# One kernel, one change: the convolution's elementwise work divided anew between VectorE and GpSimd, and four half sums given to TensorE

## The chip, the cores and the metric

One core of a Trainium2 chip runs the whole program in one launch. The metric is the device time of one execution in microseconds; the profiled execution is one more of the same kind. Engine names as in the profile: PE is TensorE (PEld its weight loads), DVE VectorE, ACT ScalarE, POOL GpSimd, SP SyncE, which here only issues DMAs. Each engine works through its own list of instructions in order; semaphores order them across engines.

## What is computed

```
_layernorm(x): (x - mean) / sqrt(var + 1e-5)                    x: [8, 256, 512] fp32
v, x1, x2 = _layernorm(x), ctx, ctx      viewed as [8, 32 heads, 8, 512]
kv[i, j] = v[i] * x2[j]                  for each head: 8 x 8 products of rows
y  = causal convolution of kv with k[head] (512 taps)  +  kv * skip[head, i]
out[j] = sum_i y[i, j] * x1[i]
x = x + tanh(g_xattn) * out
x = x + tanh(g_ffn) * MoE(_layernorm(x))    8 experts, the best one per token, 512 -> 1024 -> 512
```

The second part (routing, sorting rows by expert, the experts' matmuls) is not touched by the change. The first, here called the convolution phase, is.

## The kernel before

The convolution phase works on G = 16 groups of 128 rows (8 batches x 16 rows, that is two heads hh = 0, 1 with J = 8 rows each, L = 512 long). After a transpose time lies on the partitions in LB = 4 blocks of 128. For each group g:

- ln1 (DVE, with a square root and the scaling on ACT), then v_in: PE transposes xn into v_bank (PSUM), and ACT's v_out copies it to vT.
- outer (L325, GpSimd): kv = all 8 x 8 products of a head, 128 x 2048. kv_high (L519, ACT) rounds it to kv_hi, kv_low (L621, DVE) makes kv_lo = kv - kv_hi.
- conv (L742, PE): for each head and output block lb, 3 (lb + 1) matmuls of 128 x 512 with the head's Toeplitz strips: 30 a head, 60 a group. kv_lo of a head has to be there before its first.
- product (L634, DVE): each finished block times cT into prod, eight slices i. Eight products a group.
- The sum over i: add_pairs (L462, GpSimd, once per head) halves eight slices to four, add_fours (L664, DVE) four to two, and sum_heads (L764, PE) adds the two and the skip term by accumulating transposes into att_bank: 3 x 4.
- The skip term: skip_first (GpSimd, two operations: v times skip L440, times cK L445) gives vc, skip_sum (L670, DVE) reduces it to skip_w, skip_last (L452, GpSimd) multiplies by cT into slice J of prod. vc and skip_w exist once, not per group parity.
- residual (L642), ln2, x2_in (PE transposes), logits_of, xn2_out: the second norm and the router's logits; xn_all keeps the normed rows for the experts.

Stage g of every engine's list is written by hand in stage(g, u, n), u = g mod 2: convolution and products of g stand beside the preparation of g + 1 (outer, kv_high, kv_low, skip_first) and the end of g - 1 (sum_heads, residual, ln2). ln1 runs two groups ahead. Stages 0, 1, 14 and 15 are unrolled, 2 to 13 are a loop.

SP's list: load_x(g + 2), load_cK(g + 1), load_cT(g), load_t(g + 1) (the 1 MB of strips of a group), the store of x2, x_res. A wait in one holds all that follow.

The strips are made on the chip: k is split in k_hi (ACT) and k_lo (k_low, DVE, L614), both go to DRAM as kparts, and make_strips (L299) expands them with overlapping reads, in three parts: group 0 (4 strips, issued by SP), groups 1 to 3 (12 strips) and groups 4 to 15 (48 strips, both issued by ACT). All three wait for the kparts writes (s_kout at 48). load_t takes part 0 for group 0, part 1 for groups 1 and 2, and inside the loop the last part, so from group 3 on.

## Time and profile before

| | us |
|---|---|
| median of 3 runs | 799.68 (796.83 to 801.11) |
| profiled execution | 799.75, span 797.5 |
| PE busy | 670.8 (84% of the span) |
| POOL busy | 617.8 (77%) |
| DVE busy | 527.9 (66%) |
| ACT busy | 241.9 (30%) |

Busy tenths in 40 slices of 20 us, and the share of the 16 DMA engines:

```profile
PE   1387779888888989986781989999999999999974
DVE  4259768777777777775742999559897983650400
ACT  4123313333333333322321222333233233223320
POOL 3399979999999999991273669779888886875862
DMA  4999375555554544410496676446666664541110
```

A digit is the busy share of its slice in tenths, 9 for 90% or more. The convolution phase is slices 1 to 19, the routing follows to about 430 us, the experts run to the end.

### The profile page before, as it was taken

The page shows a single profiled execution, that of the slowest core. Times are in us where ns is not written, and L with a number is a line of the kernel's source. Part 1 is how long each engine was busy: PE and PEld are TensorE (multiplying, and loading weights), DVE is VectorE, ACT ScalarE, POOL GpSimd, SP SyncE. Part 2 cuts the span into 40 slices and gives each one's busy share as a digit, 9 for nine tenths or more (in the row PEclk, how much of TensorE's full clock was granted, in tenths as well). Part 3 has the DMA queues.
Part 4 walks back from the last instruction along what each step waited for, and adds up shares of the span by engine and source line. Part 5 has one row for each costly group of instructions (what it writes and reads, how often), then busy time and mean ns, then how long its engine had stood idle before and what let it go on. Part 6 is the DMA issues. An engine that isn't in the chain of part 4 may idle for free.

```text
span 797.5 us, 11004 instructions
## 1 busy us (share of the span) xinstructions
PE 670.8 (84%) x3136; PEld 540.1 (68%) x3137; DVE 527.9 (66%) x661; ACT 241.9 (30%) x348; POOL 617.8 (77%) x373
## 2 busy tenths in 40 slices
PE   1387779888888989986781989999999999999974
PEld 0366668666666767765671767888788888888863
DVE  4259768777777777775742999559897983650400
ACT  4123313333333333322321222333233233223320
POOL 3399979999999999991273669779888886875862
PEclk9998889999999999998696899999999999999996
DMA  4999375555554544410496676446666664541110
GB/s 136 353 347 312 133 213 145 145 145 145 145 145 145 145 145 132 118 55 26 157 223 171 231 246 222 172 143 201 208 231 201 198 223 128 188 132 41 50 51 6
DMA packets 58462, 130.63 MB, mean 164 GB/s; under 512 B 5932, under 2 KB 6124, under 8 KB 58448
## 3 DMA queue, kind: packets, MB, share of 16 engines
q1 hardware_dynamic: 43108, 96.87, 38.8%
q10 hardware_dynamic: 11020, 20.99, 8.1%
q0 software_dynamic: 4320, 12.60, 6.0%
q8 instruction: 7, 0.11, 0.1%
q14 instruction: 7, 0.06, 0.0%
HBM read 111.11 MB, written 37.67 MB: 187 GB/s over the span
## 4 chain that ended last, share of the span: by engine, by line
PE 36%; DVE 7%; POOL 3%; issue 3%; DMA 2%; ACT 0%; DVEq 0%; POOLq 0%; ACTq 0%
PE pair L1197 21%; PE bank L1210 12%; POOL sorted_x L937 2%; PE bank L1230 2%; DMA sorted_x<-xn_all,pos 1%; DVE up L1023 1%; DVE down_hi L1023 1%; DVE down_lo L1026 1%; DVE gate L1023 1%; DVE up L1026 1%; PE bank L1186 1%; DVE gate L1026 1%; DMA raw<-down_w 1%; DVE select L876 0%; POOL ys L1131 0%
## 5 line engine op out<-in xcount | busy, mean ns | idle before, releaser
L742 PE MATMUL bank<-kv_hi,strip 128*128 128x512 f32 x640 | 222.4, 415 | 24.2 <-DMA strip<-strips 22.3
L742 PEld LDWEIGHTS bank<-kv_hi,strip 128*128 128x128 f32 x640 | 125.4, 196 | 55.1 <-issue 26.2
L325 POOL TENSOR_TENSOR kv<-vT,cK 128x2048 f32<-128x2048 f32 x31 | 156.1, 5036 | 0.0
L742 PE MATMUL bank<-kv_lo,strip 128*128 128x512 f32 x320 | 131.0, 409 | 0.0
L621 DVE TENSOR_TENSOR kv_lo<-kv,kv_hi 128x2048 fp32r<-128x2048 f32 x32 | 81.5, 2548 | 51.6 <-ACT kv_hi L519 51.5
L462 POOL TENSOR_TENSOR prod<-prod 128x1024 f32<-128x1024 f32 x31 | 107.5, 3487 | 4.7 <-DVE prod L634 4.7
L1197 PE MATMUL pair<-gate,xT_hi 128*128 x304 | 98.9, 407 | 5.0 <-DVE xT_lo L1032 2.8
L1197 PE MATMUL pair<-up,xT_hi 128*128 x304 | 96.7, 399 | 2.8 <-DVE up L1026 2.8
L634 DVE TENSOR_TENSOR prod<-bank,cT 128x512 f32<-128x512 f32 x128 | 82.1, 681 | 25.4 <-DMA cT<-ctx_cols 20.7
L1023 DVE CAST down_hi<-raw 128x1024 fp32r<-128x1024 f32 x32 | 34.2, 1068 | 73.7 <-PE bank L1210 50.5
L519 ACT ACTIVATE kv_hi<-kv 128x2048 fp32r<-128x2048 f32 x32 | 61.3, 1916 | 65.8 <-POOL kv L325 54.8
L1148 POOL TENSOR_TENSOR hid<-hid,mid 128x1024 f32<-128x1024 f32 x19 | 50.1, 2638 | 31.5 <-ACT mid L1077 31.4
L742 PEld LDWEIGHTS bank<-kv_lo,strip 128*128 128x128 f32 x320 | 62.8, 196 | 11.8
L1197 PEld LDWEIGHTS pair<-up,xT_hi 128*128 128x128 f32 x304 | 57.8, 191 | 17.1 <-issue 3.2
L1197 PEld LDWEIGHTS pair<-gate,xT_hi 128*128 128x128 f32 x304 | 56.9, 192 | 18.4 <-issue 5.8
L1210 PE MATMUL bank<-down_hi,hT_hi 128*128 128x512 f32 x152 | 62.9, 414 | 6.4 <-POOL hT_lo L1158 5.7
L1210 PE MATMUL bank<-down_hi,hT_lo 128*128 128x512 f32 x152 | 61.1, 402 | 0.0
L1210 PE MATMUL bank<-down_lo,hT_hi 128*128 128x512 f32 x152 | 61.0, 401 | 0.0
L1197 PE MATMUL pair<-gate,xT_lo 128*128 x152 | 60.9, 401 | 0.0
L1197 PE MATMUL pair<-up,xT_lo 128*128 x152 | 60.6, 399 | 0.0
L1026 DVE TENSOR_TENSOR down_lo<-raw,down_hi 128x1024 fp32r<-128x1024 f32 x32 | 56.3, 1758 | 1.1
L1131 POOL TENSOR_TENSOR ys<-ys,x2s 128x512 f32<-128x512 f32 x19 | 33.5, 1761 | 25.8 <-ACT ys L1070 25.8
(149 smaller groups left out, 1131.1 us busy)
## 6 DMA issues: line engine op xcount, KB each, us to landing
strip<-strips SPq DMA_DIRECT2D x16, 1024.0 KB, 5.7
raw<-gate_w SPq DMA_DIRECT2D x32, 512.0 KB, 4.1
raw<-up_w SPq DMA_DIRECT2D x32, 512.0 KB, 4.4
raw<-down_w SPq DMA_DIRECT2D x32, 512.0 KB, 4.3
strips<-kparts ACTq DMA_DIRECT2D x1, 12288.0 KB, 74.7
sorted_x<-fill SPq DMA_DIRECT2D x14, 513.0 KB, 6.0
xs<-sorted_x ACTq DMA_DIRECT2D x20, 256.5 KB
x_in<-x_rows SPq DMA_DIRECT2D x16, 256.0 KB, 5.5
```

The lines of the kernel that those rows point to most:

```text
L325: engine.tensor_tensor(kv[:, hh, :].rearrange("p (a i j) -> p a i j", i=J, j=J), v.unsqueeze(3).broadcast_to([P, LB * NB, J, J]), c.unsque ...
L462: nc.gpsimd.tensor_tensor(terms[:, 0:J // 2], terms[:, 0:J // 2], terms[:, J // 2:J], ALU.add)\
L519: nc.scalar.activation(kv_hi[:, u, hh, :], kv[:, hh, :], ACT.Copy).then_inc(s_khi, 1)
L621: nc.vector.tensor_tensor(kv_lo[:, u, hh, :], kv[:, hh, :], kv_hi[:, u, hh, :].bitcast(f32), ALU.subtract).then_inc(s_klo, 1)
L634: nc.vector.tensor_tensor(dst[:, :, :, hh * J:(hh + 1) * J], y_bank[lb][:, :].rearrange("p (b i j) -> p b i j", i=J, j=J), c, ALU.mult).th ...
L742: last = nc.tensor.matmul(y_bank[lb][:, :], strip[:, u, 2 * hh + t, d * P:(d + 1) * P], v[:, u, hh, mb * COL:(mb + 1) * COL], start=(mb == ...
L1023: nc.vector.tensor_copy(hi, raw[:, c, :]).then_inc(s_whi, 1)
L1026: nc.vector.tensor_tensor(lo, raw[:, c, :], hi.bitcast(f32), ALU.subtract)\
L1131: nc.gpsimd.tensor_tensor(ys[:, :], ys[:, :], x2s[:, :], ALU.add).then_inc(s_add, 1)
L1148: nc.gpsimd.tensor_tensor(hid[:, :], hid[:, :], mid[:, :], ALU.mult).then_inc(s_hid, 1)
L1197: last = nc.tensor.matmul(bank[:, half * 512:(half + 1) * 512], a[:, b, :], weights[:, bass.ds(o, 512)], start=(b == 0 and n == 0), stop=( ...
L1210: last = nc.tensor.matmul(out_bank[:, :], a[:, b, :], w[:, b * 512:(b + 1) * 512], start=(b == 0 and n == 0), stop=(b == IB - 1 and n == 2))
```

## The change

kv_low goes from DVE to GpSimd; outer goes from GpSimd to DVE and reads v_bank in PSUM, so vT and v_out are gone. skip_first becomes one operation per head that reads the diagonal of kv. add_pairs is one operation for both heads, add_fours is gone, and sum_heads takes slices 0 to 3 and J: 5 x 4 transposes. skip_last(g - 1) and add_pairs(g - 1) both stand at the head of GpSimd's stage g; skip_sum(g) stands in DVE's stage g ahead of the outers of g + 1. k_low comes after both first norms. xn2 is kept twice and xn2T_out, xn2_out, ln1, v_in and x2_in change places.

```diff
-    xn2 = put("xn2", [P, L], f32, att)
+    xn2 = put("xn2", [P, 2, L], f32, att)
     xn2T = put("xn2T", [P, LB, P], f32, att)
-    vT = put("vT", [P, 2, LB * P], f32, att)
...
-        def outer_product(engine, u, hh):
...
                 def load_cK(g, u):
                     wait(eng, s_kv, 2 * (g - 1))
-                    wait(eng, s_skip, g - 1)
...
-                def outer(g, u, n, hh):
+                def skip_first(g, u, hh):
                     h = 2 * g + hh
-                    if hh == 0:
-                        eng.wait_ge(s_vT, g + 1)
-                        eng.wait_ge(s_cK[u], 16 * (n + 1))
-                    wait(eng, s_khi, h - 1)
-                    wait(eng, s_klo, h - 1)
-                    outer_product(nc.gpsimd, u, hh)
-                def skip_first(g, u):
-                    a = LB * NB
+                    eng.wait_ge(s_kv, h + 1)
                     wait(eng, s_skw, g)
-                    wait(eng, s_skip, g)
-                    s_g = skip_b[:, blk(g, 2 * J)]
-                    nc.gpsimd.tensor_tensor(
-                        vc[:, :].rearrange("p (a r) -> p a r", r=2 * J),
-                        vT[:, u, :].rearrange("p (a r) -> p a r", r=2 * J),
-                        s_g.unsqueeze(1).broadcast_to([P, a, 2 * J]), ALU.mult).then_inc(s_skv, 1)
-                    eng.wait_ge(s_skv, g + 1)
-                    nc.gpsimd.tensor_tensor(vc[:, :], vc[:, :], cK[:, u, :], ALU.mult).then_inc(s_skip, 1)
+                    v = vc[:, :].rearrange("p (a r) -> p a r", r=2 * J)[:, :, hh * J:(hh + 1) * J]
+                    same = kv[:, hh, :].rearrange("p (a d) -> p a d", d=J * J)[:, :, ::J + 1]
+                    s_g = skip_b[:, blk(g, 2 * J)][:, hh * J:(hh + 1) * J]
+                    nc.gpsimd.tensor_tensor(v, same, s_g.unsqueeze(1).broadcast_to([P, LB * NB, J]), ALU.mult)\
+                        .then_inc(s_skip, 1)
+                def kv_low(g, u, hh):
+                    h = 2 * g + hh
+                    eng.wait_ge(s_khi, h + 1)
+                    wait(eng, s_y, (h - 3) * LB)
+                    nc.gpsimd.tensor_tensor(kv_lo[:, u, hh, :], kv[:, hh, :], kv_hi[:, u, hh, :].bitcast(f32),
+                                            ALU.subtract).then_inc(s_klo, 1)
                 def skip_last(g, u, n):
...
                         skip_w[:, :, :].unsqueeze(3).broadcast_to([P, LB * NB, 2, J]), ALU.mult)\
                         .then_inc(s_skp, 1)
-                def add_pairs(g, u, hh):
-                    eng.wait_ge(s_p, (2 * g + hh + 1) * LB)
-                    terms = prod[:, u, 0:J, :].rearrange("p i (a r) -> p i a r", r=2 * J)[:, :, :, hh * J:(hh + 1) * J]
+                def add_pairs(g, u):
+                    eng.wait_ge(s_p, (g + 1) * 2 * LB)
+                    nc.gpsimd.tensor_tensor(prod[:, u, 0:J // 2, :], prod[:, u, 0:J // 2, :],
+                                            prod[:, u, J // 2:J, :], ALU.add).then_inc(s_add, 1)
+                def add_first_pairs(g, u):
+                    eng.wait_ge(s_p, g * 2 * LB + LB)
+                    terms = prod[:, u, 0:J, :].rearrange("p i (a r) -> p i a r", r=2 * J)[:, :, :, 0:J]
                     nc.gpsimd.tensor_tensor(terms[:, 0:J // 2], terms[:, 0:J // 2], terms[:, J // 2:J], ALU.add)\
                         .then_inc(s_add, 1)
-                def before_conv(g, u, n):
-                    if isinstance(g, int) and g == 0:
-                        eng.wait_ge(s_small, 32)
-                        eng.wait_ge(s_kv, 1)
-                    else:
-                        outer(g, u, n, 0)
-                    skip_first(g, u)
-                    outer(g, u, n, 1)
+                def before_conv(g, u):
+                    for hh in range(2):
+                        if isinstance(g, int) and g == 0 and hh == 0:
+                            eng.wait_ge(s_small, 32)
+                        skip_first(g, u, hh)
+                        kv_low(g, u, hh)
                 def stage(g, u, n):
                     if known(g, lambda g: g >= 1):
-                        add_pairs(g - 1, 1 - u, 1)
-                    skip_last(g, u, n)
+                        add_pairs(g - 1, 1 - u)
+                        skip_last(g - 1, 1 - u, n - 1 + u)
                     if known(g, lambda g: g < G - 1):
-                        before_conv(g + 1, 1 - u, n + u)
-                    add_pairs(g, u, 0)
-                before_conv(0, 0, 0)
+                        before_conv(g + 1, 1 - u)
+                before_conv(0, 0)
                 stages(eng, stage)
+                skip_last(G - 1, 1, G // 2 - 1)
+                add_first_pairs(G - 1, 1)
...
                 def norm2(g, u):
                     act.wait_ge(s_nb2, g + 1)
-                    wait(act, s_x2tr, g)
-                    wait(act, s_xnc, g)
-                    norm(xn2[:, :], x_res[:, u, :], rs2, nb2, s_xn2)
+                    wait(act, s_x2tr, g - 1)
+                    wait(act, s_xnc, g - 1)
+                    norm(xn2[:, u, :], x_res[:, u, :], rs2, nb2, s_xn2)
+                def xn2_out(g, u):
+                    act.wait_ge(s_xn2, g + 1)
+                    nc.scalar.activation(xn_all[:, blk(g), 0:L].rearrange("p o n -> p (o n)"), xn2[:, u, :],
+                                         ACT.Copy).then_inc(s_xnc, 1)
                 def k_high():
                     act.wait_ge(s_kin, 16)
                     nc.scalar.activation(k_hi[:, :], k_raw[:, :], ACT.Copy).then_inc(s_khalf, 1)
-                def v_out(g, u):
-                    act.wait_ge(s_vtr, g + 1)
-                    wait(act, s_kv, 2 * (g - 1))
-                    wait(act, s_skip, g - 1)
-                    nc.scalar.activation(vT[:, u, :], v_bank, ACT.Copy).then_inc(s_vT, 1)
...
                 def stage(g, u, n):
                     more = known(g, lambda g: g < G - 1)
                     before = known(g, lambda g: g >= 1)
-                    if known(g, lambda g: g < G - 2):
-                        root1(g + 2)
-                        norm1(g + 2, u)
+                    if known(g, lambda g: g >= 2):
+                        xn2T_out(g - 2)
                     if more:
                         kv_high(g + 1, 1 - u, 0)
                     if known(g, lambda g: g >= 2):
                         logits_out(g - 2)
+                    if more:
+                        kv_high(g + 1, 1 - u, 1)
                     if before:
                         root2(g - 1)
                         norm2(g - 1, 1 - u)
-                    if more:
-                        kv_high(g + 1, 1 - u, 1)
                     if known(g, lambda g: g < G - 2):
-                        v_out(g + 2, u)
+                        root1(g + 2)
+                        norm1(g + 2, u)
                     if before:
-                        xn2_out(g - 1)
-                        xn2T_out(g - 1)
...
+                def outer(g, u, n, hh):
                     h = 2 * g + hh
-                    dve.wait_ge(s_khi, h + 1)
-                    wait(dve, s_y, (h - 3) * LB)
-                    nc.vector.tensor_tensor(kv_lo[:, u, hh, :], kv[:, hh, :], kv_hi[:, u, hh, :].bitcast(f32),
-                                            ALU.subtract).then_inc(s_klo, 1)
+                    if hh == 0:
+                        dve.wait_ge(s_vtr, g + 1)
+                        dve.wait_ge(s_cK[u], 16 * (n + 1))
+                    wait(dve, s_khi, h - 1)
+                    wait(dve, s_klo, h - 1)
+                    wait(dve, s_skip, h - 1)
+                    v = v_bank.rearrange("p (a r) -> p a r", r=2 * J)[:, :, hh * J:(hh + 1) * J]
+                    c = cK[:, u, :].rearrange("p (a r) -> p a r", r=2 * J)[:, :, hh * J:(hh + 1) * J]
+                    nc.vector.tensor_tensor(
+                        kv[:, hh, :].rearrange("p (a i j) -> p a i j", i=J, j=J),
+                        v.unsqueeze(3).broadcast_to([P, LB * NB, J, J]),
+                        c.unsqueeze(2).broadcast_to([P, LB * NB, J, J]), ALU.mult).then_inc(s_kv, 1)
...
-                def add_fours(g, u):
-                    dve.wait_ge(s_add, 2 * (g + 1))
-                    nc.vector.tensor_tensor(prod[:, u, 0:2, :], prod[:, u, 0:2, :], prod[:, u, 2:4, :], ALU.add)\
-                        .then_inc(s_add2, 1)
                 def skip_sum(g):
-                    dve.wait_ge(s_skip, g + 1)
+                    dve.wait_ge(s_skip, 2 * (g + 1))
                     wait(dve, s_skp, g)
                     nc.vector.tensor_reduce(skip_w[:, :, :],
                                             vc[:, :].rearrange("p (a h i) -> p a h i", h=2, i=J), AX, ALU.add)\
...
                     before = known(g, lambda g: g >= 1)
                     product(g, u, n, 0, 0)
                     product(g, u, n, 0, 1)
-                    if before:
-                        add_fours(g - 1, 1 - u)
-                    if known(g, lambda g: g < G - 2):
-                        ln1(g + 2, u, n + 1)
+                    skip_sum(g)
+                    if more:
+                        outer(g + 1, 1 - u, n + u, 0)
                     product(g, u, n, 0, 2)
+                    if more:
+                        outer(g + 1, 1 - u, n + u, 1)
                     product(g, u, n, 0, 3)
                     if before:
                         residual(g - 1, 1 - u, n - 1 + u)
                         ln2_first(g - 1, 1 - u)
-                    if more:
-                        kv_low(g + 1, 1 - u, 0)
-                    if before:
                         ln2_last(g - 1)
                     product(g, u, n, 1, 0)
+                    if known(g, lambda g: g < G - 2):
+                        ln1(g + 2, u, n + 1)
                     product(g, u, n, 1, 1)
-                    if more:
-                        skip_sum(g + 1)
                     product(g, u, n, 1, 2)
                     product(g, u, n, 1, 3)
-                    if more:
-                        kv_low(g + 1, 1 - u, 1)
-                k_low()
                 ln1(0, 0, 0)
                 ln1(1, 1, 0)
-                dve.wait_ge(s_vT, 1)
-                dve.wait_ge(s_cK[0], 16)
-                outer_product(nc.vector, 0, 0)
-                kv_low(0, 0, 0)
-                skip_sum(0)
-                kv_low(0, 0, 1)
+                k_low()
+                outer(0, 0, 0, 0)
+                outer(0, 0, 0, 1)
                 dve.wait_ge(s_tanh, 2)
                 stages(dve, stage)
                 add_last_pairs(G - 1, 1)
-                add_fours(G - 1, 1)
...
-                    wait(pe, s_vT, g)
-                    transposes(v_bank, xn, s_vtr)
+                    wait(pe, s_kv, 2 * g)
+                    transposes(v_bank, lambda cols: xn[:, cols], s_vtr)
...
-                    pe.wait_ge(s_add2, g + 1)
+                    pe.wait_ge(s_add, G + 1 if isinstance(g, int) and g == G - 1 else g + 1)
                     pe.wait_ge(s_skp, g + 1)
                     wait(pe, s_x2, g)
-                    terms = [0, 1, J]
+                    terms = [0, 1, 2, 3, J]
...
-                    conv(g, u, n, 1, (0, 1, 2))
+                    conv(g, u, n, 1, range(LB))
                     if known(g, lambda g: g < G - 2):
                         v_in(g + 2)
-                    conv(g, u, n, 1, (3,))
                     if before:
-                        x2_in(g - 1)
+                        x2_in(g - 1, 1 - u)
```

## Rows read from the trace of the kernel before

**Rows 1.** Timeline of GpSimd, one group: start us, us, engine line op, operands, count.

```profile
169.72 1.08 POOL L452 TENSOR_TENSOR prod<-cT,skip_w 128x512 f32<-128x512 f32 x1
...
175.44 1.30 POOL L440 TENSOR_TENSOR vc<-vT,skip_b 128x512 f32<-128x512 f32 x1
...
178.06 5.78 POOL L325 TENSOR_TENSOR kv<-vT,cK 128x2048 f32<-128x2048 f32 x1
183.80 6.75 POOL L462 TENSOR_TENSOR prod<-prod 128x1024 f32<-128x1024 f32 x2
190.51 1.08 POOL L452 TENSOR_TENSOR prod<-cT,skip_w 128x512 f32<-128x512 f32 x1
```

**Rows 2.** Timeline of SP's queue, the start of the convolution phase.

```profile
4.10 0.36 SPq L393 DMA_DIRECT2D kparts<-k_lo  x1
...
7.24 0.77 SPq L299 DMA_DIRECT2D strips<-kparts  x1
21.40 0.38 SPq L357 DMA_DIRECT2D strip<-strips  x1
...
37.37 0.38 SPq L357 DMA_DIRECT2D strip<-strips  x1
...
91.03 0.38 SPq L357 DMA_DIRECT2D strip<-strips  x1
```

**Rows 3.** Timeline of ACT, its issue of strips parts 1 and 2.

```profile
14.65 7.97 ACTq L299 DMA_DIRECT2D strips<-kparts  x2
```

**Rows 4.** Timeline of DVE, 0 to 115 us; in brackets the idle time before and its releaser.

```profile
12.20 0.21 DVE L604 TENSOR_SCALAR nb<-mv,rs 128x1 f32<-128x1 f32 x1
...
36.57 1.29 DVE L634 TENSOR_TENSOR prod<-bank,cT 128x512 f32<-128x512 f32 x2 [9.20 <-DMA cT<-ctx_cols]
...
58.12 1.29 DVE L634 TENSOR_TENSOR prod<-bank,cT 128x512 f32<-128x512 f32 x2 [3.89 <-DMA cT<-ctx_cols]
...
106.28 1.29 DVE L634 TENSOR_TENSOR prod<-bank,cT 128x512 f32<-128x512 f32 x2 [7.66 <-DMA cT<-ctx_cols]
```

**Rows 5.** Four lines, each by itself: count, duration in ns (min/median/max), first and last start.

```profile
L1158 POOL TENSOR_TENSOR hT_lo<-mid,hT_hi x19: 2346/2407/3295, 442.3 to 776.5; 128x1024 fp32r<-128x1024 f32 x19
...
L325 POOL TENSOR_TENSOR kv<-vT,cK x31: 3722/4719/5788, 17.3 to 344.3; 128x2048 f32<-128x2048 f32 x31
L325 DVE TENSOR_TENSOR kv<-vT,cK x1: 2284/2284/2284, 12.3 to 12.3; 128x2048 f32<-128x2048 f32 x1
...
L519 ACT ACTIVATE kv_hi<-kv x32: 1899/1918/1926, 14.6 to 350.1; 128x2048 fp32r<-128x2048 f32 x32
...
L670 DVE TENSOR_REDUCE skip_w<-vc x16: 670/676/679, 19.4 to 347.9; 128x64 f32<-128x512 f32 x16
```

**Rows 6.** Timeline of DVE beside rows 1.

```profile
177.65 2.60 DVE L621 TENSOR_TENSOR kv_lo<-kv,kv_hi 128x2048 fp32r<-128x2048 f32 x1 [0.96 <-ACT kv_hi L519]
```

**Rows 7.** Timeline of PE: transposes, 18 matmuls, transposes.

```profile
82.97 1.48 PE L764 MATMUL pair<-ident,prod 128*128 128x128 f32 x12
84.20 0.48 PE L742 MATMUL bank<-kv_hi,strip 128*128 128x512 f32 x1
...
88.49 0.60 PE L722 MATMUL pair<-ident,xn 128*128 128x128 f32 x4
```

**Rows 8.** Windows: length, busy us of five engines, then PE clock, DMA share, GB/s.

```profile
12.00:16.00 4.00, 1.11 (x4) 0.71 (x4) 2.58 (x3) 2.17 (x2) 1.23 (x1) 1.00 0.26 100
85.00:90.00 5.00, 5.00 (x25) 4.08 (x24) 3.95 (x7) 2.07 (x3) 4.92 (x4) 1.00 0.15 58
```

**Rows 9.** Timeline of DVE, the end of the convolution phase.

```profile
367.54 0.69 DVE L634 TENSOR_TENSOR prod<-bank,cT 128x512 f32<-128x512 f32 x1 [2.13 <-PE bank L742]
...
369.60 1.22 DVE L664 TENSOR_TENSOR prod<-prod 128x1024 f32<-128x1024 f32 x1
```

**Rows 10.** Timeline of PE, the same stretch.

```profile
370.88 2.26 PE L764 MATMUL pair<-ident,prod 128*128 128x128 f32 x12 [1.19 <-DVE prod L664]
```

**Rows 11.** Timeline of ACT, the same stretch.

```profile
380.49 0.62 ACT L538 ACTIVATE xn_all<-xn 128x512 f32<-128x512 f32 x1
```

More of the change, by code:

```diff
@@ L534, in xn2T_out @@
                         .then_inc(s_xn2T, 1)
-                def xn2_out(g):
-                    act.wait_ge(s_xn2, g + 1)
-                    nc.scalar.activation(xn_all[:, blk(g), 0:L].rearrange("p o n -> p (o n)"), xn2[:, :], ACT.Copy)\
-                        .then_inc(s_xnc, 1)
                 def stage(g, u, n):
@@ L569, in _ @@
                 norm1(0, 0)
-                v_out(0, 0)
                 root1(1)
@@ L573, in _ @@
                 kv_high(0, 0, 0)
-                v_out(1, 1)
                 make_strips(act, 1)
@@ L578, in _ @@
                 stages(act, stage)
+                xn2T_out(G - 2)
                 logits_out(G - 2)
@@ L582, in _ @@
                 xn2T_out(G - 1)
+                xn2_out(G - 1, 1)
                 logits_out(G - 1)
-                xn2_out(G - 1)
             @block.vector
```

22 lines of the change are left out of this document (7 added, 15 removed).

## The prediction

> **What bounds the kernel now.** I read the page's busy shares and slices first: PE is busiest, and the chain that ended last is PE almost throughout from 500 us on, but none of that is code that the change touches. The change lies in the convolution phase, up to 381 us, so I read the timeline of each engine there. GpSimd (POOL) never stops in the loop: an add_pairs for each head, skip_last, outer, two vc products, outer, and again, every 20.79 us (190.51 less 169.72) [rows 1]. So a group costs what GpSimd's queue costs.
>
> The loop doesn't run freely from the start. Before it stand DMAs: the expanded strips are written to DRAM in three parts, part 0 issued by SP at 7.24 and landed at 21.40, when SP goes on to load strip(0); parts 1 and 2 issued by ACT from 14.65; part 2 landed at 91.03, when SP goes on to strip(3) [rows 2, 3]. Behind strip(3) in SP's queue stands cT(3), and DVE starts group 3's products with it at 106.28 [rows 4]. From there GpSimd sets the time of 12 groups (3 to 15).
>
> **GpSimd's new queue.** It loses two outers and two vc products of 512, and gets two kv_low of 2048 and two skip_first of 256 elements a partition; its two add_pairs of 1024 become one of 2048. Durations: a 1024-element GpSimd subtraction takes 2.35 when nothing delays it, 512 take 1.30 [rows 1, 5], so 2.1 ns an element and 0.2 fixed: 4.52 for 2048, about 4.48 from start to next start; 256 elements 0.70. Bounds for 2048: 3.72 (the outer, with broadcast operands) and 5.79 (its longest) [rows 5]; the 1024 row is the very operation of kv_low, so I go by it. New queue: 3 x 4.48 + 1.08 + 2 x 0.70 = 15.9 us a group, 4.9 less than now.
>
> Is the undelayed duration the right one? The outer takes 3.72 or up to 5.79, and the long one at 178.06 runs into DVE's kv_lo (177.65 for 2.60, alone 2.28): 178.06 to 180.25 is overlap, and 3.6 is left [rows 1, 5, 6]. So one waits for the other. After the change DVE has no operation in the loop with two SBUF inputs left: outer and product each take one from PSUM. The Trainium skill (SBUF — State Buffer, "Who interferes with whom") says the same: a DVE instruction with two SBUF inputs and a GpSimd one that reads SBUF exclude each other, one with a single SBUF input excludes nobody. The trace agrees.
>
> **Why 15.9 isn't the period.** DVE's skip_sum(g) overwrites skip_w, so it waits for s_skp at g: skip_last(g-1). In the old code GpSimd does skip_last(g) at the start of stage g; now add_pairs(g-1) and skip_last(g-1) both stand in stage g, add_pairs first. And skip_sum(g) is now ahead of both outers of the next group in DVE's queue. That closes a ring over three engines. From the start of add_pairs(g-1), called A: add_pairs 4.48, skip_last 1.08; skip_sum 0.59 (0.68, less the overlap with what follows); outer for head 0 at 2.28 (the one that DVE does now; it reads SBUF, but a product from PSUM is no slower than its size: two of 512 in 1.29); kv_high 1.92; then kv_low 4.48, skip_first 0.70, kv_low 4.48, and the next add_pairs [rows 1, 4, 5]. Three hand-overs between engines are 0.21 in all, an estimate (one from DVE to PE is 0.06: add_fours ends at 370.82, PE starts at 370.88 [rows 9, 10]). Sum 20.22 us. GpSimd idles some 4.3 of it, waiting for kv_high of head 0. The new period is 20.22 against 20.79: 0.57 x 11 = 6.3 us, not the 54 that the queue alone would promise.
>
> Other engines in this ring: DVE after skip_sum has two outers, two products, residual, two norms and four products, some 13 us, so it ends near A + 19, inside the period. PE: 18 matmuls take 4.29, so 60 take 14.3; twelve transposes take 1.23, so twenty 2.05; with two sets of four transposes (0.6 at most each) and the logits about 18 us [rows 7]. The eight added transposes (0.8 us) vanish in PE's idle time. sum_heads comes about 6.2 after A and finds skip_last done at 5.6. Dropping add_fours frees DVE and takes away a wait of PE, but neither is in the ring: nothing gained there. ACT loses v_out and has room.
>
> Bounds of the period: skip_first reads the diagonal of kv with a step of 36 bytes, which no GpSimd row shows; nearest are 0.70 by size and 1.30 as for 512. The Trainium skill (GPSIMD Engine Reference, "Performance pitfalls for Q7 kernels") speaks against it: reads with a step over 8 bytes cost about one cycle an element more. By it 256 elements would add about 0.2 us (an estimate), 11 groups 2.3 us, and the sum below would be 801.3. No run here shows it. For the period I keep both ends: 17.9 (2048 elements at 3.72) and 21.0 (skip_first 1.3, outer 2.5); the long end of 5.79 is the exclusion, which is gone.
>
> **The start, where the change gives time back.** k_low is moved on DVE from the very front to behind ln1(0) and ln1(1). Those wait for ACT's first square root; the last of ln1(1) starts at 12.20 now, and without ACT's v_out ahead of the second square root at about 10.7, an estimate; its ends are 10 and 12.2. So k_low runs at 10.8, SP's kparts<-k_lo goes from 4.10 to 11.5, and make_strips(0), 3.14 behind it, from 7.24 to 14.66 [rows 2, 4]: 7.4 late. ACT's parts 1 and 2 wait for the same but left at 14.65 anyway [rows 3]: unmoved. Part 0 now competes from its first byte.
>
> What that is worth hangs on the DMA engines. While part 0 runs alone the share is 0.26 at 100 GB/s, four of 16 engines; at the end of part 2, 85 to 90 us, the share is 0.15: two or three engines work on while the others are done [rows 8]. If the last ones are part 0's four, the work they don't do before 14.66 comes at their end, and 91.03 becomes 98.4. The Trainium skill (DMA: Bandwidth & Descriptors, "Why a DMA increments its semaphore by 16 and not by 1") has the rule: a transfer whose slowest dimension is 4 or 12 long uses the lowest-numbered 4 or 12 engines. By it the last are part 0's; otherwise nothing shifts. The trace's 0.26 and its straggling end agree with the rule. I take the shift: cT(3) and the products of group 3 at 106.28 + 7.42 = 113.7, the next skip_sum could start at 114.9 (two products, 1.21).
>
> There is a second way to be late. Part 0 lands later: alone it took 14.2 us from issue, which would be 28.8; at half rate it is 37. I take 35.5. SP's strip(0), x_in, cK, cT follow: 15.2 us from SP's issue to the first product now (21.40 to 36.57), 20.7 when the engines are full (37.37 to 58.12, with one load more) [rows 2, 4]. I take 17.5: the first product at 53.0 instead of 36.6. From there the ring runs: 1.21, then skip_sum to second kv_low 14.63, two periods 40.4, add_pairs and skip_last 5.6: skip_last(2) ends 61.8 later, at 114.8. Both ways meet at 114.9. (Today there is slack here: DVE waits 7.66 us for cT(3) [rows 4].) Then add_pairs(3) starts at 114.9 + 14.63 = 129.5.
>
> **The sum.** Eleven periods: add_pairs(14) at 129.5 + 222.4 = 351.9; skip_last(14) ends at 357.5; sum_heads(14) 2.05 to 359.6; the last 30 matmuls 7.15; the last product starts at 366.9 instead of 367.54 [rows 9]. Tail: add_fours 1.2 less; eight more transposes at the pace of that place (twelve took 2.26) 1.5 more; ACT's xn2_out, 0.62, goes ahead of logits_out and leaves the end, 0.5 less [rows 9 to 11]: -0.2. Together -0.8. The rest of the program is unchanged. The profiled execution took 799.75 us around a span of 797.5, close to the median of 799.68, so the forecast is **799.0 us**: no change, the gain of the period (6.3, and about 2 from the first cycle) eaten by the start.
>
> **Rivals.**
> - Faster, the start is free: the straggling engines are others, and part 0 lands before 28. Then group 3 begins at 106.28 as now, which needs the first product by 45.6; add_pairs(3) at 122.1, and the time is 791.6. For it: the strip loads have slack of tens of us now. Against: share 0.26 and the thin end of the transfer. 0.17.
> - Faster, PE is the bound: skip_last isn't what skip_sum waits for in time. PE's 18.2 a group instead of 20.2 gives 799.0 - 11 x 2.0 = 777. The code's order speaks against it. 0.04; a ring that is shorter because GpSimd's 2048s take 4.1 would be 3 x 0.38 x 11 = 13 less, 786. 0.06.
> - Slower, the start: SP's first loads, in the full DMA. If part 0 lands at 38 and cT(0) 20.7 behind it, the first product is at 58.7, skip_last(2) ends at 120.5 and everything is 5.6 later: 804.6. It decides from a first product at about 57.2, when it passes 803. 0.17.
> - Slower, the ring: the strided skip_first at 1.3 and an outer from PSUM at 2.5 give 21.0, 11 x 0.8 = 9 more: 808. It decides from 20.6. 0.10.
>
> **How the numbers follow.** What can be told from no change here is 0.5%, 4 us. The forecast's case, 795.5 to 803 by itself, holds 0.46. Faster by over 0.5%: 0.27; within: 0.46; slower: 0.27. The range of 8 in 10 reaches to the first and third rival and half into the fourth: 791 to 807.
>
> **What would show it.** In the changed profile: DVE idle before skip_sum, ended by GpSimd's skip_last, some 4 us in each group; GpSimd idle 2.9 before the first skip_first, ended by DVE's outer, and 1.4 before the first kv_low, ended by ACT; periods of 20.2 between add_pairs; GpSimd's 2048s at 4.5 with little spread; SP's part 0 at 14.7, part 2 landed at 98; the first product near 53; the last near 367. I am wrong if add_pairs come every 18 us (the ring isn't closed), if group 3's products start at 106 (the start is free), or if kv_low stretches well over 4.6.

## The result, and the profile after

The changed kernel takes 806.65 us (median of 12 runs, 804.81 to 808.59) against 798.75 for the kernel before (12 runs, 796.80 to 804.24): ratio 1.0094, 95% interval 1.0075 to 1.0113. The forecast was 799.0, "no change". The time lies just inside the upper end of the range, 791 to 807, but the kernel became slower, by 0.9%, and that is clear of the measurement's uncertainty where the forecast had said no change.

The profiled execution of the changed kernel took 805.02 around a span of 802.9. Its busy times and the count of instructions (page, part 1; span in the first line):

```profile
span 802.9 us, 11207 instructions
...
PE 677.2 (84%) x3264; PEld 554.8 (69%) x3265; DVE 485.9 (61%) x644; ACT 238.2 (30%) x332; POOL 558.3 (70%) x359
```

PE's 3264 matmuls hold the 128 added transposes (16 groups of 8; with 12 a group there are 3136). No engine is full in the convolution phase. What fills a group is read from the timelines. GpSimd, one group (counterpart of [rows 1]; in brackets idle time before the operation and who ended it):

```profile
234.06 4.63 POOL L444 TENSOR_TENSOR prod<-prod 128x2048 f32<-128x2048 f32 x1
238.59 1.15 POOL L435 TENSOR_TENSOR prod<-cT,skip_w 128x512 f32<-128x512 f32 x1
242.91 0.91 POOL L420 TENSOR_TENSOR vc<-kv,skip_b 128x256 f32<-128x256 f32 x1 [3.17 <-DVE kv L608]
244.94 4.63 POOL L427 TENSOR_TENSOR kv_lo<-kv,kv_hi 128x2048 fp32r<-128x2048 f32 x1 [1.12 <-ACT kv_hi L506]
249.52 0.82 POOL L420 TENSOR_TENSOR vc<-kv,skip_b 128x256 f32<-128x256 f32 x1
250.30 4.56 POOL L427 TENSOR_TENSOR kv_lo<-kv,kv_hi 128x2048 fp32r<-128x2048 f32 x1
254.83 4.58 POOL L444 TENSOR_TENSOR prod<-prod 128x2048 f32<-128x2048 f32 x1
```

DVE beside it (counterpart of [rows 6]):

```profile
239.84 0.69 DVE L653 TENSOR_REDUCE skip_w<-vc 128x64 f32<-128x512 f32 x1 [4.61 <-POOL prod L435]
240.45 2.28 DVE L608 TENSOR_TENSOR kv<-pair,cK 128x2048 f32<-128x2048 f32 x1
...
250.92 1.88 DVE L623 TENSOR_TENSOR prod<-bank,cT 128x512 f32<-128x512 f32 x3
```

The last row holds the last three products of the group; they end at 252.80. ACT beside it:

```profile
242.85 1.93 ACT L506 ACTIVATE kv_hi<-kv 128x2048 fp32r<-128x2048 f32 x1 [9.81 <-DVE kv L608]
```

Follow the releasers: skip_sum (239.84) had to wait 4.61 us for skip_last; GpSimd's skip_first (242.91) for DVE's outer; kv_low (244.94) for ACT's kv_high. So the ring of the forecast is closed, with GpSimd idle for 4.29 us of it (3.17 + 1.12; forecast 4.3), and a group takes 254.83 - 234.06 = 20.77 us: as much as before (20.79). DVE's waits say how often (engine, line, waited for: us, times, longest):

```profile
DVE skip_w L653 <- POOL prod L435: 63.6, 15, 7.4
```

The start. SP's queue (counterpart of [rows 2]):

```profile
13.37 0.77 SPq L296 DMA_DIRECT2D strips<-kparts  x1
...
97.94 0.38 SPq L344 DMA_DIRECT2D strip<-strips  x1
```

DVE there (counterpart of [rows 4]):

```profile
11.05 0.67 DVE L594 TENSOR_TENSOR k_lo<-k_raw,k_hi 32x512 fp32r<-32x512 f32 x1
...
52.09 1.29 DVE L623 TENSOR_TENSOR prod<-bank,cT 128x512 f32<-128x512 f32 x2 [35.98 <-DMA cT<-ctx_cols]
...
112.42 1.29 DVE L623 TENSOR_TENSOR prod<-bank,cT 128x512 f32<-128x512 f32 x2 [5.04 <-DMA cT<-ctx_cols]
115.29 0.69 DVE L653 TENSOR_REDUCE skip_w<-vc 128x64 f32<-128x512 f32 x1 [1.57 <-POOL prod L435]
```

k_low runs at 11.05 and what stands behind it is late: strips part 0 by 6.1 us, strip(3) by 6.9, group 3's first product by 6.1 (106.28 before). But these products are not what holds group 3 up: skip_sum(3), at 115.29, has waited 1.57 us more for skip_last(2), the end of the second group's way round the ring. The end of the phase, DVE (counterpart of [rows 9]):

```profile
373.58 0.69 DVE L623 TENSOR_TENSOR prod<-bank,cT 128x512 f32<-128x512 f32 x1 [2.13 <-PE bank L716]
```

PE there (counterpart of [rows 10]):

```profile
375.66 2.40 PE L738 MATMUL pair<-ident,prod 128*128 128x128 f32 x20
```

The last product is 6.0 us later than the 367.54 of before, the routing behind it 4.4 (it starts at 385.83, against 381.43), and the span is 5.4 longer. The medians are 7.9 apart: the profiled execution of the changed kernel (805.02) is a quick one of its runs, that of before (799.75) is not. Windows around those transposes (length; busy us of PE, PEld, DVE, ACT, POOL; PE clock, DMA share, GB/s), in the changed kernel:

```profile
375.60:378.10 2.50, 2.46 (x22) 2.20 (x21) 0.00 (x2) 0.18 (x1) 0.00 (x0) 1.00 0.00 0
```

In the kernel before:

```profile
370.80:373.20 2.40, 2.26 (x12) 1.86 (x12) 0.04 (x2) 0.00 (x0) 0.00 (x0) 0.65 0.00 0
```

Twenty transposes at the full granted clock (2.4 GHz) take 2.40 us; twelve took 2.26 with the granted clock at 0.65 over the stretch, so between its two levels.

### The profile page after: what moved, and what is told of

Read it like the earlier page. It is cut to its first block, busy times and chain, and to the rows that moved or that the text cites. A ratio compares the mean times of both kernels' runs of the same rounds, so it can differ in the third digit from the quotient of the medians.

```text
span 802.9 us, 11207 instructions
## 1 busy us (share of the span) xinstructions
PE 677.2 (84%) x3264; PEld 554.8 (69%) x3265; DVE 485.9 (61%) x644; ACT 238.2 (30%) x332; POOL 558.3 (70%) x359
## 4 chain that ended last, share of the span: by engine, by line
PE 36%; DVE 7%; POOL 3%; issue 2%; DMA 2%; ACT 0%; POOLq 0%; DVEq 0%; ACTq 0%
PE pair L1170 22%; PE bank L1183 12%; POOL sorted_x L910 2%; PE bank L1203 2%; DMA sorted_x<-xn_all,pos 1%; DVE up L999 1%; DVE up L996 1%; DVE down_hi L996 1%; DVE down_lo L999 1%; PE bank L1159 1%; DVE gate L999 1%; DVE gate L996 1%; DMA raw<-down_w 1%; DVE select L849 0%; POOL ys L1104 0%
## 5 line engine op out<-in xcount | busy, mean ns | idle before, releaser
L716 PE MATMUL bank<-kv_hi,strip 128*128 128x512 f32 x640 | 216.7, 409 | 30.7 <-DMA strip<-strips 30.7
L427 POOL TENSOR_TENSOR kv_lo<-kv,kv_hi 128x2048 fp32r<-128x2048 f32 x32 | 147.3, 4602 | 23.1 <-ACT kv_hi L506 19.7
L623 DVE TENSOR_TENSOR prod<-bank,cT 128x512 f32<-128x512 f32 x128 | 84.6, 684 | 75.0 <-DMA cT<-ctx_cols 43.4
L1170 PE MATMUL pair<-gate,xT_hi 128*128 x304 | 101.1, 415 | 4.8 <-DVE xT_lo L1005 2.6
L420 POOL TENSOR_TENSOR vc<-kv,skip_b 128x256 f32<-128x256 f32 x32 | 28.3, 883 | 80.4 <-DVE kv L608 67.5
L608 DVE TENSOR_TENSOR kv<-pair,cK 128x2048 f32<-128x2048 f32 x32 | 72.9, 2281 | 0.0
L1170 PEld LDWEIGHTS pair<-gate,xT_hi 128*128 128x128 f32 x304 | 58.3, 197 | 18.6 <-issue 5.6
L1170 PEld LDWEIGHTS pair<-up,xT_hi 128*128 128x128 f32 x304 | 57.8, 191 | 17.2 <-issue 3.2
L444 POOL TENSOR_TENSOR prod<-prod 128x2048 f32<-128x2048 f32 x15 | 69.1, 4604 | 0.0
L696 PE MATMUL pair<-ident,xn 128*128 128x128 f32 x128 | 21.2, 313 | 46.1 <-ACT xn L480 41.3
```

The source lines that it names most:

```text
L420: nc.gpsimd.tensor_tensor(v, same, s_g.unsqueeze(1).broadcast_to([P, LB * NB, J]), ALU.mult)\
L427: nc.gpsimd.tensor_tensor(kv_lo[:, u, hh, :], kv[:, hh, :], kv_hi[:, u, hh, :].bitcast(f32), ALU.subtract).then_inc(s_klo, 1)
L444: nc.gpsimd.tensor_tensor(prod[:, u, 0:J // 2, :], prod[:, u, 0:J // 2, :], prod[:, u, J // 2:J, :], ALU.add).then_inc(s_add, 1)
L608: nc.vector.tensor_tensor(kv[:, hh, :].rearrange("p (a i j) -> p a i j", i=J, j=J), v.unsqueeze(3).broadcast_to([P, LB * NB, J, J]), c.uns ...
L623: nc.vector.tensor_tensor(dst[:, :, :, hh * J:(hh + 1) * J], y_bank[lb][:, :].rearrange("p (b i j) -> p b i j", i=J, j=J), c, ALU.mult).th ...
L716: last = nc.tensor.matmul(y_bank[lb][:, :], strip[:, u, 2 * hh + t, d * P:(d + 1) * P], v[:, u, hh, mb * COL:(mb + 1) * COL], start=(mb == ...
```

## The experiments

Theory: two separate things. **Ring**: skip_last behind add_pairs closes the ring, which costs what GpSimd's shorter queue should have given. **Start**: k_low behind the two norms makes strips part 0, the last strips and everything behind them late by 7 us. The rivals: that the period is set by something else (GpSimd's operations themselves, TensorE), and that the start is hidden. Four kernels separate them.

**k_low first.** In the changed kernel:

```diff
+                k_low()
                 ln1(0, 0, 0)
                 ln1(1, 1, 0)
-                k_low()
```

> The changed kernel with k_low back at the front of DVE's list, nothing else. Theory START (part 0 of the strips leaves 6 us later, the four DMA engines that carry it finish last, and so group 3 begins later): strip(3) is issued at about 91 instead of 97.9, group 3's products start at 106 instead of 112.4, add_pairs(3) at 122.5 instead of 130.2, the period stays 20.76; 799.0 us, 7.7 below the changed kernel's 806.65, and no different from the kernel before. Rival NO-START (the time is lost in the loop alone, the strips have slack): 806 us, group 3 still near 112.

Measured: 796.44 us (793.65 to 802.04, 10 runs; before 800.16; ratio 0.9962, 0.9930 to 0.9993). Its SP queue:

```profile
7.42 0.77 SPq L296 DMA_DIRECT2D strips<-kparts  x1
...
88.76 0.38 SPq L344 DMA_DIRECT2D strip<-strips  x1
```

Its DVE:

```profile
103.76 1.29 DVE L623 TENSOR_TENSOR prod<-bank,cT 128x512 f32<-128x512 f32 x2 [5.17 <-DMA cT<-ctx_cols]
```

Part 0 goes at 7.42 and strip(3) 9.2 us earlier than in the changed kernel, and the time falls by 10. The wait before skip_sum stays (62.2 us in 15). Without its late start the change is no slower than before, barely faster.

By which way the start costs its time is in the same view:

```profile
43.27 1.29 DVE L623 TENSOR_TENSOR prod<-bank,cT 128x512 f32<-128x512 f32 x2 [27.35 <-PE bank L716]
...
106.44 0.69 DVE L653 TENSOR_REDUCE skip_w<-vc 128x64 f32<-128x512 f32 x1 [1.39 <-POOL prod L435]
```

Here too skip_sum(3) waits last for skip_last(2), not for strip(3). The first product is 8.8 us earlier than in the changed kernel (52.09) and skip_sum(3) 8.9 (115.29). So with this ring it is the late first cycle (part 0, strip(0), the first product) that costs the time; the late strip(3) costs nothing of its own. The theory had charged it to the last strips.

**skip_last ahead of add_pairs.** In the changed kernel:

```diff
+                        skip_last(g - 1, 1 - u, n - 1 + u)
                         add_pairs(g - 1, 1 - u)
-                        skip_last(g - 1, 1 - u, n - 1 + u)
```

> The changed kernel with skip_last(g-1) ahead of add_pairs(g-1) in GpSimd's stage, nothing else: the same work on every engine. Theory RING (skip_sum waits for skip_last, which waits for add_pairs; the ring of 20.76 contains add_pairs, 4.53): the ring falls to 16.2, GpSimd's queue of 16.6 and PE's sum of about 18.2 are longer, so PE sets the period at 18.2 to 18.6; 11 x 2.4 = 26 us and some at the start: 776 to 781 us. DVE's idle time before skip_sum (63.6 us now) nearly goes. Rival QUEUE (GpSimd as such is too slow, its order doesn't matter): 805 to 807.

Measured: 772.55 us (771.54 to 774.93, 4 runs; ratio 0.9643, 0.9595 to 0.9692). Its GpSimd timeline, one group:

```profile
202.07 1.10 POOL L435 TENSOR_TENSOR prod<-cT,skip_w 128x512 f32<-128x512 f32 x1
...
208.07 0.96 POOL L420 TENSOR_TENSOR vc<-kv,skip_b 128x256 f32<-128x256 f32 x1 [0.34 <-DVE kv L608]
...
220.06 1.10 POOL L435 TENSOR_TENSOR prod<-cT,skip_w 128x512 f32<-128x512 f32 x1
```

17.99 us from skip_last to skip_last, and no wait before skip_sum is left. Two swapped lines are worth 34 us by the medians (30.1 between the profiled executions, 28.7 of it at the last product, 344.91 against 373.58): the ring is shown. The time lies 3.5 us below the 776 to 781 that was expected, because TensorE's group takes 17.99 and not 18.2 to 18.6.

**Both.**

> Both of these edits together (k_low first, skip_last ahead of add_pairs). START and RING both right and independent: 769 to 773 us. If only RING: 778. If only START: 799. If the two overlap (with the short period the early groups catch up and wait for strip(3) in any case) then between 769 and 776.

Measured: 763.86 us (760.43 to 764.99, 4 runs; ratio 0.9528, 0.9474 to 0.9582). The window of one group:

```profile
234.00:251.99 17.99, 17.99 (x98) 15.13 (x97) 13.64 (x25) 7.06 (x9) 16.56 (x6) 1.00 0.54 160
```

PE is busy for 17.99 of 17.99: the bound has gone over to TensorE. The start is worth 8.7 us here, so the two causes add up. (The 769 to 773 expected for that case was built on the same 18.2 to 18.6 a group.)

**k_low late in the kernel before.**

```diff
-                k_low()
                 ln1(0, 0, 0)
                 ln1(1, 1, 0)
+                k_low()
```

> The kernel before with k_low moved behind both first norms on DVE, nothing else. Here ACT's v_out delays the second norm, so k_low runs at 12.4 and the kparts are complete near 16.3 instead of 7.2: part 0 is 9 us late and parts 1 and 2 are 1.6 late. START: strip(3) issued at 98 to 101 instead of 91, everything from group 3 on 7 to 10 us later: 806 to 809 us. NO-START: 799, as before.

Measured: 809.83 us (808.46 to 810.98, 4 runs; ratio 1.0107, 1.0056 to 1.0159). Its SP queue:

```profile
98.75 0.38 SPq L357 DMA_DIRECT2D strip<-strips  x1
```

Its DVE:

```profile
113.71 1.29 DVE L634 TENSOR_TENSOR prod<-bank,cT 128x512 f32<-128x512 f32 x2 [0.27 <-DMA cT<-ctx_cols]
```

Alone, in the old code, the moved k_low makes the kernel slower by as much as the whole change does. DVE's wait for cT(3), behind strip(3), is down to 0.27 us here, from 7.66: strip(3) and the first cycle are late together.

What was open then: why the ring is 20.77 and not 20.22, what the third part of the change (no second tree level) does, and whether the end of the strips is set by part 0's engines.

**skip_first without the step.** It reads `[:, :, 0:J]` in place of `[:, :, ::J + 1]`.

> The changed kernel, with skip_first reading the first eight of each 64 elements of kv instead of the diagonal (so another quantity is summed; sizes, waits and engines are the same). Theory (the step of 36 bytes costs 0.15 to 0.2 us an instruction, and the ring is closed, so that the one skip_first that lies in it counts once a group): skip_first goes from a median of 0.88 us to about 0.70, skip_last comes every 20.6 us instead of 20.76, the time is 2 us below the changed kernel's 806.7, so 804.7. Rival (256 elements cost 0.88 whatever their step, a fixed cost): skip_first stays at 0.88 and the time at 806.7.

Measured, GpSimd's timeline:

```profile
199.73 0.75 POOL L420 TENSOR_TENSOR vc<-kv,skip_b 128x256 f32<-128x256 f32 x1 [3.17 <-DVE kv L608]
...
220.34 0.75 POOL L420 TENSOR_TENSOR vc<-kv,skip_b 128x256 f32<-128x256 f32 x1 [3.17 <-DVE kv L608]
```

An instruction takes 0.73 instead of 0.88 us (means of 32) and the group 20.61 instead of 20.77: the step costs 0.15 us, once in the ring. The last product starts at 372.66 (373.58). The time of the whole program, 838.92 us, can't be read: other values send other tokens to the experts, and TensorE has 3432 matmuls where the changed kernel has 3264.

**The second tree level put back into the changed kernel.**

```diff
+                    if before:
+                        add_fours(g - 1, 1 - u)
...
-                    terms = [0, 1, 2, 3, J]
+                    terms = [0, 1, J]
```

(add_fours stands behind product(0,2), and sum_heads waits for it.)

> The changed kernel with the second tree level put back: DVE adds half sums 2 and 3 to 0 and 1 (1024 elements) behind the third product of the stage, and TensorE takes two half sums and the skip term, 12 transposes instead of 20. Theory (neither engine is in the ring over GpSimd, DVE and ACT; DVE runs add_fours between two operations while GpSimd is waiting for kv_high or starting kv_low): TensorE is 0.8 us less busy a group, the ring stays near 20.8, the time is 806.7 within 3; perhaps 1 less at the end of the phase. Rival (an addition of two SBUF operands on DVE shuts GpSimd out, or is shut out by it): GpSimd's operation beside it stretches by up to 1.2 us, the ring is 22.0, 11 groups give 13 more, 820.

Measured: 814.92 us (814.34 to 818.51, 4 runs; ratio 1.0213, 1.0153 to 1.0273), 8 more than the changed kernel. Neither theory had the mechanism. GpSimd:

```profile
219.18 4.61 POOL L445 TENSOR_TENSOR prod<-prod 128x2048 f32<-128x2048 f32 x1 [0.83 <-DVE prod L624]
...
240.92 4.61 POOL L445 TENSOR_TENSOR prod<-prod 128x2048 f32<-128x2048 f32 x1 [0.90 <-DVE prod L624]
```

DVE:

```profile
240.15 0.69 DVE L624 TENSOR_TENSOR prod<-bank,cT 128x512 f32<-128x512 f32 x1 [1.04 <-PE bank L725]
```

PE, in this group and in one that is not stretched:

```profile
166.55 1.53 PE L747 MATMUL pair<-ident,prod 128*128 128x128 f32 x12 [3.16 <-DVE prod L653]
...
229.98 2.82 PE L747 MATMUL pair<-ident,prod 128*128 128x128 f32 x12 [2.83 <-DVE prod L653]
```

GpSimd's operations are not stretched, but in this group add_pairs waits for the last product, and the group takes 21.74. There is a second ring, and it goes over TensorE: skip_last lets DVE start skip_sum; add_fours (228.33, 1.59 us) stands behind it; PE's sum_heads waits for add_fours (2.83 us here); head 1's 30 matmuls stand behind sum_heads; their last product lets GpSimd start add_pairs, and that is ahead of the next skip_last. This ring is the longer one in the loop only where PE's granted clock fell to its lower level (1.2 GHz) over sum_heads or the matmuls behind it. From 229.90 to 232.50 the clock is 0.50, and from the start of the twelve transposes to the next matmul 2.48 us pass; in the group of 251.71 the clock is 1.00 and they take 1.29. From add_pairs(3) at 134.94 on, four of eleven groups take 21.7 to 21.8, the others 20.7 to 20.9, all after a wait of 2.8 to 3.2 us. In the changed kernel sum_heads follows head 0's matmuls without a wait (240.14), and the last product ends 2.0 us ahead of add_pairs (252.80, 254.83). Of the 11.4 us that the last product is later than in the changed kernel (384.95 against 373.58), 4.7 are there at add_pairs(3), 4.5 come in the eleven groups and 2.2 behind them. The first 4.7 come with three such waits of add_pairs, 1.34, 2.16 and 0.89 us.

**Only the third part, in the kernel before**: add_fours removed, `terms = [0, 1, 2, 3, J]`, sum_heads waits for both add_pairs.

> The kernel before with only the third part of the change: no add_fours on DVE, TensorE's sum_heads takes four half sums and the skip term (20 transposes instead of 12). Theory (in the kernel before add_fours, an addition of two SBUF operands, starts 0.1 us after GpSimd's add_pairs and stretches the outer behind it from 3.72 to 4.72 in each group): the outer is 3.7, GpSimd's period 19.8 instead of 20.79, 12 periods give 12 less: 787. Rival (what the prediction on record assumed of this part in the changed kernel: no ring or queue that bounds has it, so nothing is gained): 799, less at most 1; or, with TensorE bounding, which is 17.9 of 20.79 now and 18.7 then, no more than that.

Measured: 784.94 us (782.5 to 787.5, 4 runs; ratio 0.9813, 0.9767 to 0.9860). The expectation was made from two rows of the kernel before, add_fours on DVE's timeline

```profile
169.80 2.09 DVE L664 TENSOR_TENSOR prod<-prod 128x1024 f32<-128x1024 f32 x1 [1.05 <-POOL prod L462]
```

and the outer beside it on GpSimd's:

```profile
170.76 4.72 POOL L325 TENSOR_TENSOR kv<-vT,cK 128x2048 f32<-128x2048 f32 x1
```

GpSimd's timeline without add_fours:

```profile
182.08 1.09 POOL L451 TENSOR_TENSOR prod<-cT,skip_w 128x512 f32<-128x512 f32 x1
183.13 3.73 POOL L324 TENSOR_TENSOR kv<-vT,cK 128x2048 f32<-128x2048 f32 x1
...
201.88 1.08 POOL L451 TENSOR_TENSOR prod<-cT,skip_w 128x512 f32<-128x512 f32 x1
```

The outer is 3.73 instead of 4.72 and the group 19.80 instead of 20.79. In the kernel before this part alone takes off 15 us (1.9%). The profiled executions, 17.2 apart, show 12.9 in the twelve groups from skip_last(3) on (250.46 against 237.61 us), and 3.4 ahead of them: strip(3) was loaded at 88.12 here, at 91.03 before, and DVE waits for it in both. That load varies by as much between kernels with the same start, so those 3.4 are not shown to be the part's own. In the whole change the group is not 1 us shorter for it, because the ring sets the group.

**The second level where TensorE bounds** (on "both"):

> The kernel with k_low first and skip_last ahead of add_pairs (763.9), with the second tree level put back on DVE, 12 transposes instead of 20. Theory (TensorE is the bound there, 17.99 us busy of 17.99 in a group): eight transposes, 0.8 us, less in each group, period 17.2, 12 groups give 10 less: 754. Rival (DVE's addition of two SBUF operands shuts GpSimd out for its 1.2 us, and GpSimd's 16.6 a group plus its small waits then bounds): period 17.8 to 18, the time 761 to 764; GpSimd's subtraction or skip_first beside add_fours stretches by about 1.2 in the trace.

Measured: 762.03 us (761.97 to 769.54, 4 runs; ratio 0.9569, 0.9498 to 0.9639). GpSimd, one group:

```profile
207.52 1.09 POOL L436 TENSOR_TENSOR prod<-cT,skip_w 128x512 f32<-128x512 f32 x1
...
215.19 4.62 POOL L428 TENSOR_TENSOR kv_lo<-kv,kv_hi 128x2048 fp32r<-128x2048 f32 x1 [1.09 <-ACT kv_hi L507]
...
225.20 1.07 POOL L436 TENSOR_TENSOR prod<-cT,skip_w 128x512 f32<-128x512 f32 x1
```

DVE's add_fours stands at 213.50 for 1.69. The window of the group:

```profile
207.52:225.20 17.68, 17.61 (x90) 14.21 (x89) 15.07 (x25) 7.09 (x10) 16.58 (x7) 1.00 0.62 163
```

17.68 instead of 17.99, where 17.2 was expected. GpSimd is not what bounds: it waits some 1.1 us for kv_high in every group, and from 150 to 320 us only one wait of another engine, 1.6 us, is ended by GpSimd. PE has no room: eight transposes less are 0.8 us, but it pauses about 0.1 us ahead of sum_heads, which waits for add_fours, and 0.2 ahead of the transposes at 223.85 (starts 0.35 and 0.45 apart, where its matmuls start 0.24 apart), for which ACT delivers xn late, at the end of DVE's stage. So the loop runs over PE and DVE (product(0,1) at 209.50, then DVE nearly without a pause to the norm that ACT's xn waits for, the transposes, the next products), and add_fours lengthens it. add_fours beside GpSimd takes 1.69, alone 1.22 [rows 9]; GpSimd's skip_first beside it is not stretched. So nearly the rival's period came (17.8 to 18 expected), with the lock paid by DVE and not by GpSimd. That PE and DVE set it is read from one trace; no run takes it apart. Both kernels once more, side by side:

> The changed kernel with k_low first and skip_last ahead of add_pairs, once more, beside the same with the second tree level. TensorE bounds it at 17.99 a group: 763.9 as in its first run, within 2.

> The same with the second tree level on DVE, once more. Theory (GpSimd's queue of 16.6 and its wait of 1.09 for kv_high bound it at 17.68 a group, 0.31 under TensorE's 17.99 without the second level; the tail has add_fours more and eight transposes less): 12 groups give 3.5 less than the run beside it, 0.4%. Rival (the difference is taken back by the first groups and the tail): no difference that the interval tells from nothing.

Measured: 765.55 (760.72 to 768.97) without and 763.56 (760.43 to 768.29) with the second level, 6 runs each; ratios to before 0.9560 (0.9515 to 0.9606) and 0.9544 (0.9503 to 0.9584). The intervals overlap: no difference that can be told. Either beats both kernels by over 4%.

**Strips in parts of 16, 16 and 32 rows.** `STRIP_PARTS = [range(4), range(4, 8), range(8, G)]` in the changed kernel.

> The changed kernel with the strips cut into parts of 16, 16 and 32 rows instead of 4, 12 and 48; all else the same. Theory (a transfer whose slowest dimension is 4 or 12 long works on 4 or 12 engines only, and these are the stragglers at the end): the load of strip(3) starts well before the 97.9 of the changed kernel, at about 85, and the DMA share shows no thin stretch of 0.2 to 0.5 ahead of it; part 0 is four times as large, so strip(0) starts later than 34.9, near 42, and the time of the first product moves from 52.1 to about 59. The start then ends by the way over the first cycle: about 5 us more in all, 812. Rival (the straggling has to do with the order of the parts in the queues, not with their row counts): strip(3)'s load stays at 97 to 98, thin stretch included, and the time does not fall.

Measured: 830.98 us (828.36 to 832.18, 4 runs; ratio 1.0392, 1.0332 to 1.0451). Windows:

```profile
12.00:16.00 4.00, 0.00 (x0) 0.00 (x0) 4.00 (x2) 2.27 (x2) 0.34 (x1) 1.00 0.60 134
85.00:90.00 5.00, 5.00 (x23) 3.97 (x22) 3.47 (x10) 2.67 (x3) 5.00 (x3) 1.00 0.26 101
```

The last part lands at 94.0 (issued at 14.6, landed 79.4 later), 3.7 us before that of the changed kernel (97.7) where the theory wanted 13, and a thin stretch is still ahead of it (share 0.26). So what makes the end thin is not only that 4 and 12 rows fall on few engines; that theory is not borne out. strip(3) itself is loaded at 109.22, not at the 85 expected, because the first cycle is so late. At the beginning the share is 0.60, in the changed kernel 0.32 in the same window; from 13.5 to 14.0, with part 0 issued at 13.4 in both and ACT's parts only from 13.9 on, it is 0.49 against 0.26. That 4 rows keep few engines busy stands. And I priced the first cycle wrong: part 0, four times as large, landed at 53.8 (expected 42), the first product was at 77.8 (expected 59), and the time 19 us over my figure.

## Why the prediction was wrong

- **What bounds before, GpSimd's new queue**: right, a little short in size. Its operations come to 3 x 4.60 + 1.09 + 2 x 0.88 = 16.65 us a group, 15.9 forecast. The outers on DVE took 2.27 to 2.29, so reading PSUM and SBUF costs as the row said.
- **The ring, the failed step.** The mechanism was right; the term "the new period is 20.22" was mis-sized. By pieces, forecast and measured:

```
add_pairs                          4.48   4.53
skip_last, to skip_sum's start     1.08   1.25
skip_sum, to outer's start         0.59   0.61
outer, to kv_high's start          2.28   2.40
kv_high, to kv_low's start         1.92   2.09
kv_low                             4.48   4.58
skip_first                         0.70   0.78
kv_low                             4.48   4.53
three hand-overs                   0.21   (in the rows above)
sum                               20.22  20.77
```

  No piece is far off: 0.20 too little for the three operations of 2048, 0.08 for skip_first, 0.07 for skip_last, 0.17 for the hand-overs (0.10, 0.12 and 0.16, where 0.21 in all was taken from a single DVE-to-PE row), 0.03 for the rest. But the gain was a difference of two numbers of 20, and 0.55 of error took the whole 0.57. The 6.3 us that were to pay for the late start did not come, so the start's 6 us remained. Eleven periods make 6.0 us; with 0.7 at the start that is all that the last product is late against the forecast (373.58 against 366.9). The case of the ring being slower stood in the prediction with 0.10, "decides from 20.6"; it measured 20.77. The Trainium skill's rule for skip_first (GPSIMD Engine Reference, "Performance pitfalls for Q7 kernels", about one cycle more an element for a step over 8 bytes) held: the diagonal costs 0.15 us more than the same 256 elements in a row, 0.2 by the rule (an estimate). I weighed it, and left it out of the sum.
- **The lock**: right. After the change nothing on DVE in the loop reads two operands from SBUF, and GpSimd's 2048s spread over 0.17 us only (4.49 to 4.66), where the outers spread from 3.72 to 5.79 [rows 5]. The Trainium skill (SBUF — State Buffer, "Who interferes with whom") agrees with this, and with what add_fours and GpSimd do to each other in the experiments.
- **"Dropping add_fours: nothing gained there"**: wrong as a statement on this part. It is true of the ring that I drew, and DVE does end inside the period, at A + 18.7 (252.80) where I had A + 19. But the "wait of PE" that I set aside closes a second ring over sum_heads and head 1's matmuls. Put back, add_fours makes PE wait 2.8 to 3.2 us a group; where the granted clock is at 0.50 behind that wait, the group takes 21.7, and the kernel is 8 us slower (814.92). In the kernel before it held up GpSimd's outer by 1.0 a group, which was in its rows of DVE and GpSimd side by side, and I looked there only for kv_low's collision.
- **The start**: nearly right in size; of the two ways that were to meet at 114.9, one bound. skip_last(2) ended at 115.19 (114.8 forecast) and held skip_sum(3) for 1.57 us; over strip(3) alone it could have started at 113.7. With the short ring it is the other way: on "both" DVE waits 10.6 us for cT(3), behind strip(3). Forecast and measured: strips part 0 14.66, 13.37; first product 53.0, 52.09; strip(3) 98.4, 97.94; group 3's products 113.7, 112.42; add_pairs(3) 129.5, 130.22. With the strips in their old parts, seven profiles with k_low first load strip(3) at 86.4 to 91.0, five with it late at 94.2 to 99.5. That it is late because part 0's own engines are the last is not shown: with 16 rows a part the thin end remained. The Trainium skill (DMA: Bandwidth & Descriptors, "Why a DMA increments its semaphore by 16 and not by 1") says only which engines a transfer uses, the lowest-numbered 4 or 12 here; that these finish last was my inference from it. What makes the thin end stays open.
- **The tail**: 1.4 us better than forecast. Twenty transposes took 2.40 us at a granted clock of 1.00, where the twelve of before had 2.26 at 0.65; I had counted eight more at the old pace, 1.5.
- **The sum**, against the forecast's 799.0: +0.7 at the start, +6.0 in the ring, -1.4 in the tail is 804.3; the profiled execution took 805.02. The remaining 0.7 is in code that the change doesn't touch, and the median, 806.65, lies 1.6 above this execution.

## What to carry over

A gain that is the difference between two nearly equal periods is worth no more than the error of the longer sum: here twenty microseconds of ring, each piece within 0.2 us, had an error as large as the gain. When an edit takes work off the busiest engine, look first for the instruction that the next engine waits for and ask what stands ahead of it in its queue: the order of two calls was worth 34 us here. Work that is off the ring can still make an engine wait, and so close another ring: follow the wait on, as the "wait of PE" was not followed here. And test the parts of a change one by one: one part alone gave 15 us, one took 10, and the whole, with both in it, lost 8.

## What the hardware showed

- An addition of two SBUF operands on DVE and GpSimd's work hinder one another, and either can be the one that pays: in the kernel before, GpSimd's outer went from 3.73 to 4.72 beside add_fours (which took 2.09); in the kernel with the second level on "both", add_fours took 1.69 instead of 1.22 and GpSimd's operation nothing more. Both times the operation that had started first kept its time: skip_last, at 169.72, took its 1.08, add_fours (169.80) ended at 171.89, and the outer (170.76) got the 1 us more.
- From the end of one engine's operation to the start of the next on another engine: DVE to ACT 0.12 us (240.45 + 2.28 to 242.85), ACT to GpSimd 0.16 (242.85 + 1.93 to 244.94), GpSimd to DVE 0.10 (238.59 + 1.15 to 239.84).
- The same transposes cost 0.12 us each at the full granted clock, with the router's matmuls just ahead of them, and 0.19 at 0.65, after PE had stood idle for 1.19 us [rows 10]. In the changed kernel with add_fours put back PE stood idle for 2.8 to 3.2 us ahead of them in every group of the loop; the granted clock behind it was 1.00 in some groups and 0.50 in others, and twelve of them took 1.29 or 2.48 us to the next matmul.
